# Real and imaginary parts on the same partitions, and a new passage between the two stages, in a two-block convolution kernel

## What is computed

```python
x = x + L0(_gn(x))    # per image: attention over 4 weight sets, 3x3 depthwise conv, 32x32 channel mix
x = x + L1(_gn(x))

# L1, with p = 8:
hidden = einsum('oc,bchw->bohw', w_hidden, x)            # 32 -> 192 channels
hidden = depthwise_conv_3x3(hidden, w_dw)
q, k, v = split(hidden, 3, axis=1)                       # 64 channels each
q_fft, k_fft = rfft2(8x8 patches of q), rfft2(8x8 patches of k)
out = irfft2(q_fft * k_fft)                              # circular convolution, patch by patch
out_norm = layernorm over the 64 channels of out, times norm_w plus norm_b
result = einsum('oc,bchw->bohw', w_out, v * out_norm)    # 64 -> 32 channels
```

## Time and profile before

| | us |
|---|---|
| median of 3 runs | 2588.41 (2576.62 to 2591.29) |
| the profiled execution: its own time | 2588.67 |
| its span in the profile | 2586.9 |
| PE busy | 2465.4 (95%) |
| DVE busy | 1638.6 (63%) |
| ACT busy | 1432.4 (55%) |
| mean granted share of PE's clock | 0.972 |

### The profile page before, as it was taken

One profiled execution on the slowest core, in us unless ns is written; L12 is line 12 of the kernel. 1 busy time (PEld: TensorE's weight loads), 2 busy tenths in 40 slices (PEclk: granted clock), 3 DMA queues, 4 the chain that ended last, 5 costly groups with the idle time before them and its releaser, 6 DMA issues.

```text
span 2586.9 us, 90657 instructions
## 1 busy us (share of the span) xinstructions
PE 2465.4 (95%) x40199; PEld 1644.8 (64%) x40199; DVE 1638.6 (63%) x4058; ACT 1432.4 (55%) x2381; POOL 476.5 (18%) x324
## 2 busy tenths in 40 slices
PE   6888988969999999999999999999999999999998
PEld 3333333357777777777777777777777777777775
DVE  3566766536666666666666666666666666666665
ACT  3455656555555555555555555555555555555552
POOL 1000000002222222222222222222222222222222
PEclk9888889879999999999999999999999999999999
DMA  7588898762222222222222222222222222233222
GB/s 139 147 210 214 219 237 215 195 155 69 68 69 69 69 69 68 69 69 69 69 68 69 69 69 69 68 69 69 69 69 68 69 69 68 71 74 74 72 52 50
DMA packets 60345, 248.30 MB, mean 96 GB/s; under 512 B 12393, under 2 KB 12658, under 8 KB 53714
## 3 DMA queue, kind: packets, MB, share of 16 engines
q1 hardware_dynamic: 59954, 242.50, 38.5%
HBM read 140.74 MB, written 101.72 MB: 94 GB/s over the span
## 4 chain that ended last, share of the span: by engine, by line
PE 76%; issue 1%; ACT 1%; DVE 0%; SPq 0%; DMA 0%; ACTq 0%
PE bank L575 21%; PE bank L652 18%; PE bank L668 10%; PE bank L558 9%; PE bank L635 8%; PE bank L588 6%; PE bank L597 4%; ACT arena L821 1%; SPq L318 0%; DMA xn_d<-arena 0%; DVE arena L1110 0%; DVE arena L961 0%; ACT arena L866 0%; DVE arena L1198 0%; DVE arena L1135 0%
## 5 line engine op out<-in xcount | busy, mean ns | idle before, releaser
L441 POOL TENSOR_TENSOR arena<-arena 128x8 f32<-128x8 f32 x256 | 452.2, 1766 | 1585.1 <-DVE arena L1116 1580.1
L575 PE MATMUL bank<-arena 128*64 128x512 f16 x4608 | 689.3, 393 | 0.0
L812 ACT ACTIVATE arena<-bank 100x512 f32<-100x512 f32 x1024 | 604.2, 628 | 95.8 <-PE bank L558 74.4
L1198 DVE TENSOR_TENSOR arena<-bank,arena 128x512 f32<-128x512 f32 x512 | 352.8, 691 | 432.3 <-PE bank L652 352.4
L652 PE MATMUL bank<-arena 100*64 100x128 f32 x8192 | 511.6, 274 | 13.7 <-issue 7.0
L652 PEld LDWEIGHTS bank<-arena 100*64 100x64 f32 x8192 | 455.9, 136 | 52.6 <-issue 45.6
L558 PEld LDWEIGHTS bank<-arena 128*36 128x36 f16 (+1 forms) x8192 | 327.8, 104 | 228.0 <-ACT arena L812 12.7
L512 PE MATMUL bank<-arena 32*32 32x508 f32 (+1 forms) x9216 | 391.7, 665 | 52.6 <-issue 37.7
L558 PE MATMUL bank<-arena 128*36 128x128 f16 (+1 forms) x8192 | 388.9, 220 | 11.0 <-DVE arena L1100 4.2
L858 ACT ACTIVATE arena<-bank 128x512 f32<-128x512 f32 x256 | 149.3, 598 | 343.8 <-PE bank L635 261.7
L821 ACT ACTIVATE arena<-bank,arena 128x256 f32<-128x256 f32 x512 | 261.0, 560 | 128.5 <-PE bank L588 127.9
(11 more groups left out here) (112 smaller groups left out, 1624.1 us busy)
## 6 DMA issues: line engine op xcount, KB each, us to landing
arena<-xn_d SPq DMA_DIRECT2D x128, 536.2 KB, 8.2
xn_d<-arena SPq DMA_DIRECT2D x130, 260.0 KB, 4.5
x_d<-arena SPq DMA_DIRECT2D x64, 512.0 KB, 8.3
arena<-x_d SPq DMA_DIRECT2D x128, 256.0 KB, 4.9
out<-arena SPq DMA_DIRECT2D x128, 256.0 KB, 5.4
arena<-x_in SPq DMA_DIRECT2D x32, 544.0 KB, 10.1
arena<-x_in SPq DMA_DIRECT2D x32, 528.0 KB, 10.0
arena<-spectra_in SPq DMA_DIRECT2D x1, 1152.0 KB
```

What stands on the lines that cost most here:

```text
L441: pool.tensor_tensor(tiny["rstd"][:, slot], tiny["var_eps"][:, slot], powers, ALU.pow).then_inc(s_root, 1)
L575: mm = pe.matmul(v_banks[chunk % 3][64 * s:64 * s + 64, :], v_w[:, 64 * tap:64 * tap + 64], at(xs[half], row * WP + 32 * k + dx, [32 * WP, ...
L812: act.activation(h_rows[0:WIN, :, first:first + 4], banks[g % ring][0:WIN, :].rearrange("p (i c) -> p c i", i=4), ACT.Copy).then_inc(s_h_r ...
L1198: dve.tensor_tensor(parts(prod[m % 3][:, 512 * second:512 * second + 512]), parts(k_banks[n % 3]), q_sb[m % 2][:, 256 * second:256 * secon ...
```

## The change

**Layout.** A real 8 x 8 patch has 64 independent real numbers as its spectrum. The new constants keep just these: row r of the first 32 and row r of the second 32 are the real and the imaginary part of one frequency (four rows hold purely real frequencies). So q and k both have 64 numbers a channel, in two parts of 32. In both octets a channel is two matmuls of 32 columns, and four channels stand beside each other on the four blocks of 32 partitions. Real and imaginary part of a channel stand on the same partitions, in different columns. DVE multiplies all four pairings (real by real, imaginary by real and so on) with instructions of the same size and number, 16 a unit. The inverse sums four matmuls of 32 rows instead of two of 64 rows, on four row tiles by two column tiles, for 16 channels at a time, into four banks. `G_k` and the table `spectra` are smaller, and `transform_step` makes 16 matmuls instead of 24.

**Order in the spectral part.** The k octet m now stands before q octet m+1. There is one q bank instead of two, and q octet m+1 waits until ACT has copied q octet m. There are two k banks of an octet each instead of three of a quad each. `project(tail, 3)` stands after q octet 2. `v_chunk(u, half, 0, 0, ...)` stands between the last k octet and the last inverse. ACT copies each inverse out in four pieces of 256 columns instead of two of 512, and does `turned_out(tail, 3, 1)` behind its first q copy instead of ahead of it. DVE does `gate(tail, 3, 1)` behind the first two products.

**Passage.** `high(14)` and `low(14)` stand ahead of unit 0's hidden work and of its first four windows. DVE's wait for the stores is gone, since the buffers of the spectral part no longer lie on the images' halves. The two `high(15)` are apart on ACT, and `load_xs(0, 1)` is issued earlier.

```diff
@@ PE, spectral part @@
-                    if positive(8 * u + m - 1):
-                        pe.wait_ge(s_q_copied, 8 * u + m - 1)
-                    for pair in range(4):
-                        for par in range(2):
-                            ch = 8 * m + 2 * pair + par
-                            mm = pe.matmul(banks[m % 2][64 * par:64 * par + 64, 128 * pair:128 * pair + 128],
-                                           G_q[0:WIN, 64 * ch:64 * ch + 64], hwin[0:WIN, 128 * ch:128 * ch + 128], start=True, stop=True)
+                    if positive(8 * u + m):
+                        pe.wait_ge(s_q_copied, 8 * u + m)
+                    for quad in range(2):
+                        for part in range(2):
+                            for c in range(4):
+                                ch, first = 8 * m + 4 * quad + c, 256 * quad + 128 * part
+                                mm = pe.matmul(q_bank[32 * c:32 * c + 32, first:first + 128],
+                                               G_q[0:WIN, 64 * ch + 32 * part:64 * ch + 32 * part + 32],
+                                               hwin[0:WIN, 128 * ch:128 * ch + 128], start=True, stop=True)
...
-                def inverse_octet(m):
-                    for part in range(2):
-                        for par in range(2):
+                def inverse(e):
+                    pe.wait_ge(s_prod_ready, 16 * u + 4 * e + 4)
+                    if positive(16 * u + 4 * e):
+                        pe.wait_ge(s_y_ready, 16 * u + 4 * e)
...
+                    for both in range(4):
+                        for c in range(4):
                             for lam in range(2):
-                                mm = pe.matmul(i_banks[par][64 * lam:64 * lam + 64, 256 * (m % 2):256 * (m % 2) + 256],
+                                mm = pe.matmul(i_banks[c][64 * lam:64 * lam + 64, 256 * (e % 2):256 * (e % 2) + 256],
...
@@ PE, hidden_group @@
-                if g < 2 and positive(8 * u):
-                    pe.wait_ge(s_q_copied, 8 * u)
+                if g == 0 and positive(16 * u):
+                    pe.wait_ge(s_prod_ready, 16 * u)
+                if g in (1, 2) and positive(16 * u):
+                    pe.wait_ge(s_y_ready, 16 * u - (3, 1)[g - 1])
@@ ACT, inverse_out @@
-                for par in range(2):
-                    act.activation(Y_out[:, 16 * e + par:16 * e + 16:2, :, :],
-                                   i_banks[par].rearrange("p (c s j) -> p c s j", s=2, j=32), ACT.Copy).then_inc(s_y_ready, 1)
+                if u == 0 and e == 0:
+                    act.wait_ge(s_xl_ready, 4 * NB)
...
+                for c in range(4):
+                    act.activation(Y_out[:, 16 * e + c:16 * e + 16:4, :, :],
+                                   i_banks[c][:, 256 * (e % 2):256 * (e % 2) + 256].rearrange("p (c s j) -> p c s j", s=2, j=32),
+                                   ACT.Copy).then_inc(s_y_ready, 1)
@@ DVE, before unit 0 @@
-            dve.wait_ge(s_xn_out, 128 * NB)
             spectral(0, None, (1, 1, 0))
```

More of the change, by code:

```diff
@@ L240, in build @@
         xq = [take(BAND * W) for _ in range(3)]
-        x2_1, x2_2, x2_0 = [take(QPIX) for _ in range(3)]
+        x2_1, x2_2 = [take(QPIX) for _ in range(2)]
+        conv_w = [take(9 * 32) for _ in range(2)]
+        first_image_free = top[0]
+        x2_0 = take(QPIX)
         x2 = [x2_0, x2_1, x2_2]
@@ L251, in build @@
         ones_row = take(128)
-        conv_w = [take(9 * 32) for _ in range(2)]
         st1, st2 = take(6 * NCH), take(6 * NCH)
@@ L352, in _ @@
                     load_x(later, (2, 3))
+                if b == NB + 1:
+                    load_xs(0, 1)
                 if older is not None:
@@ L557, in hidden_group @@
                     for low, high in ((0, 64), (64, WIN)):
-                        mm = pe.matmul(banks[g % ring][low:high, 128 * i:128 * i + 128], w[:, first + low:first + high], hidden_w,
+                        mm = pe.matmul(ring[g % len(ring)][low:high, 128 * i:128 * i + 128], w[:, first + low:first + high], hidden_w,
                                        start=True, stop=True)
@@ L637, in q_octet, with k_octet @@
                     mm.then_inc(s_q_mm, 1)
-                def k_quad(n, octet=None):
-                    if positive(16 * u + n - 2):
-                        pe.wait_ge(s_prod_ready, 16 * u + n - 2)
-                    if n == 1 and tail is not None:
+                def k_octet(m):
+                    if positive(16 * u + 2 * m - 2):
+                        pe.wait_ge(s_prod_ready, 16 * u + 2 * m - 2)
+                    if m == 0 and tail is not None:
                         pe.wait_ge(s_gated, 8 * u - 1)
-                    if n == 2 and tail is not None:
-                        pe.wait_ge(s_t_copied, 8 * u)
-                    for pair in range(2):
+                    for quad in range(2):
@@ L647, in k_quad @@
                         for part in range(2):
-                            if octet is not None and pair == 1 and part == 1:
-                                inverse_inputs(octet)
-                            for par in range(2):
-                                ch = 4 * n + 2 * pair + par
-                                mm = pe.matmul(k_banks[n % 3][64 * par:64 * par + 64, 256 * part + 128 * pair:256 * part + 128 * pair + 128],
-                                               G_k[0:WIN, 128 * ch + 64 * part:128 * ch + 64 * part + 64],
+                            for c in range(4):
+                                ch, first = 8 * m + 4 * quad + c, 256 * quad + 128 * part
+                                mm = pe.matmul(k_banks[m % 2][32 * c:32 * c + 32, first:first + 128],
+                                               G_k[0:WIN, 64 * ch + 32 * part:64 * ch + 32 * part + 32],
@@ L851, in spectral @@
             def spectral(u, tail):
-                if tail is not None:
-                    turned_out(tail, 3, 1)
                 for m in range(8):
@@ L857, in spectral @@
                         act.wait_ge(s_prod_ready, 16 * u + 2 * m - 2)
-                    act.activation(q_sb[m % 2], banks[m % 2], ACT.Copy).then_inc(s_q_copied, 1)
-                    if m % 2 == 1 and m >= 3:
+                    act.activation(q_sb[m % 2], q_bank, ACT.Copy).then_inc(s_q_copied, 1)
+                    if m == 0 and tail is not None:
+                        turned_out(tail, 3, 1)
+                    if m in (3, 5, 7):
                         inverse_out(u, m // 2 - 1)
@@ L1088, in _ @@
                 first_stats(later, range(3, NCH))
+            for i in range(4):
+                low(NB - 2, i)
             Y4 = Y.rearrange("p (s c j) -> p s c j", s=2, j=32)
```

179 lines of the change are left out of this document (86 added, 93 removed).

## The result

The changed kernel takes 2666.98 us (median of 4 runs, 2657.29 to 2687.61) against 2584.86 for the kernel before (4 runs): ratio 1.033, 95% interval 1.026 to 1.040. It is slower by 82 us at the medians. The profiled execution of the changed kernel is its longest run, 2687.61 us (span 2685.8), 99 us over the profiled one of before.

The account below looks back on a forecast made before the run. PE bounds the kernel, busy 95% of the span. Units at 59.2 + 7.4 us against 63.1 (+105), unit 31 -3.6, unit 0's turn +0.9, passage -11, start -9 gave +82 on 2588.7: 2670 us, range 2525 to 2765.

Parts of the forecast that it names:

- instructions come in time: Rival for stage 2: a late packet hides or the load lets packets in; 59.2 us a unit, 2449 us; chance 0.16.
- Octets and inverse: Spectral part: k octets 0.87 us instead of 1.75, 7.0 us a unit gained; q octets and inverse as before.
- The 36 ns of the earlier trace: Rival, spectral part: four column tiles at 36 ns a matmul, +6.4 us a unit of work, 2775 us; chance 0.05.
- the 62 ns: Sequencer cost per MATMUL by a skill rule: 47.6 us for the spectral part's 768 matmuls; given no chance.
- Spectral part without late packets: First q octet to last inverse: 31.3 - 7.0 + 2.2 + 0.4 = 26.9 us.
- Last inverse to turn: ACT's start on the last inverse to first turn: 6.8 us instead of 5.9, as ACT's copies take longer.
- Stand: Early in units 1 to 30: PE waits 4.8 us for a late instruction packet, from 7.2 to 12.0 us.
- Packets behind it: Instruction packets after the unit's late one stay tight: +0.5 us a unit, between 0 and 2.
- Clock: Half clock around each wait of PE loses 2.6 us a unit, between 0 and 5.1; rival, clock holds: 2593, chance 0.18.
- the waits swallowed: Spectral part: 0.5 us a unit of waits for ACT's copies, absorbed by PE's wait for the late packet.
- Start and passage: Start: fewer transforms and loads, -9 us (4 to 11). Passage: unit 0's spectral part ends 11 us earlier (5 to 16).
- Unit 31 and the end: The last unit, taken to have no load and so no late packets: -3.6 us.

Follow-up runs that it names:

- e4: Changed kernel without load_xs in units 1 to 30, which compute on the first two half images again; 2522.0 us, 0.976 of the kernel before.
- e7: Changed kernel with all transfers of a unit cut and spread, a second residual buffer and windows 0 to 3 later; 2420.9 us, 0.935 of the kernel before.
- e8: Kernel before, with PE waiting in each unit behind the first q octet for a chain of 13 small POOL memsets; 2799.6 us, ratio 1.082.
- e9: Changed kernel with only the residual's transfers moved (second residual buffer, store and load in pairs in the front); 2612.0 us, 1.009 of the kernel before.
- e1: Changed kernel with load_xs's 4 transfers cut into 16 pieces at the same place; 2575.2 us, 0.995 of the kernel before.
- e2: Changed kernel with load_xs in two parts, the second released after v's first chunk; 2544.8 us, 0.983 of the kernel before.
- e6: Kernel before, with two more transfers of 536 KB, which nobody reads, behind load_xs in each unit; 2589.6 us, ratio 1.000.
- e11: Kernel before, with two more transfers of 536 KB, which nobody reads, ahead of load_xs; 2588.7 us, ratio 1.001.

## Why the prediction was right

**Bound and mechanism.** Forecast 2670, measured 2667, by the mechanism named: packets late behind `load_xs`, the clock falling with the stand (e4, e7 and e8 show it). That the number is met within 3 us is partly luck: the terms below are read in the profiled execution, 2687.6 us, where +98.9 stands against the +82 forecast, and several terms missed in opposite directions. The rival "instructions come in time" (2449) is what e7 reaches by another edit.

**Octets and inverse.** Taken: 0.87 us an octet, 1.9 an inverse. Measured: 0.87 and 1.93 (899.59 to 901.52 in e7). The 36 ns of the earlier trace rows don't hold for four column tiles over 100 rows, so that rival falls. So do the 62 ns that the prediction takes from the Trainium skill for decoding in firmware: 32 recorded matmuls in 0.87 us are 27 ns each.

**Spectral part without late packets.** Sum 26.9 us, measured 26.9 in e7's unit 6.

**Last inverse to turn.** Taken 6.8, measured 5.8 (1641.80 to 1647.57): timeline of ACT in unit 16 of the changed kernel.

```profile
1641.80 1.21 ACT L870 ACTIVATE arena<-bank 128x256 f32<-128x256 f32 x4 [3.91 <-PE bank L679]
```

The step that failed is the price of a piece of 256 columns, taken as at most 0.51 us from `turned_out`: four together took 1.21 and not 2.04. DVE's statistics start at 1643.05, 1.25 us behind ACT's start and not 2.0, which is 0.75 of the 1.0; from there to the turn there are 4.5 us where 4.8 were taken, and why is open. Turn to q0: 25.5 as taken.

**Stand.** Taken: PE at the packet's end after 7.2 us, usable at 12.0, stand 4.8. In units 11 to 15 PE is there at 7.1 on average and goes on at 11.0: 3.9; over units 1 to 30 it is 7.5, 11.5 and 4.0. The mis-sized term is 12.0: in one unit of the five (11) PE could go on at 7.5 already. **Packets behind it**: taken 0.5, measured 1.3 (idle time of the changed kernel less that of e9); I had not counted the residual's transfers. **Clock**: taken 2.6, measured 3.3. Together with the waits swallowed 7.4 taken; 66.9 - 58.6 = 8.3 measured. And 59.2 without late packets was 58.6 in e7, mainly by the turn. The misses have opposite signs: 59.2 + 7.4 = 66.6 foreseen, 58.6 + 8.3 = 66.9 measured.

**Start and passage.** Timelines of the changed kernel: first convolution; DVE's first product of unit 0; a stand of PE in unit 0 and the inverse behind it; the hidden group behind the last inverse.

```profile
41.84 5.50 PE L522 MATMUL bank<-arena 32*32 32x512 f32 x160 [0.75 <-ACT arena L775]
```

```profile
544.34 1.28 DVE L1201 TENSOR_TENSOR arena<-bank,arena 128x512 f32<-128x512 f32 x2
```

```profile
563.76 1.08 PE L650 MATMUL bank<-arena 100*32 100x128 f32 x14 [2.63 <-issue]
564.77 3.72 PE L679 MATMUL bank<-arena 32*64 32x256 f32 x64
```

```profile
574.22 0.41 PE L570 MATMUL bank<-arena 128*64 128x128 f16 x8
```

Against the earlier trace rows: -9.8 for the start (9 taken), -19.7 at the first product, and -17.6 at the end of unit 0's spectral part, so -7.8 for the passage (11 taken, between 5 and 16). The first product came 9.9 us earlier by the passage, where I had taken 7; the step that failed is "unit 0 runs on warm". PE stood 2.63 us in it for nothing that the profile shows, and the inverse behind the stand took 3.72 us in place of 1.93. These sizes are those of one execution, though. Unit 1's first q octet comes at 605.7 here (623.4 before, -17.7), and at 592.5 to 601.7 in e1, e2, e4, e7 and e9, which have the same stage 1, passage and order: there start and passage together brought 22 to 31 us where 20 were taken.

**Unit 31 and the end.** Taken -3.6, measured +2.6. Timeline of PE in unit 31 (first q octet at 2612.59), in its third inverse and then behind the last one:

```profile
2634.98 3.24 PE L679 MATMUL bank<-arena 32*64 32x256 f32 x49 [1.91 <-issue]
```

```profile
2649.29 1.12 PE L602 MATMUL bank<-arena 128*128 128x128 f32 x4 [2.80 <-DVE arena L1137]
2650.34 4.05 PE L589 MATMUL bank<-arena 128*64 128x512 f16 x18
```

The last inverse ends 30.8 us after the first q octet and not 26.9: unit 31 has no `load_xs`, but it has the residual's transfers, and PE stands 1.91 us at 20.5 us and works slower behind it. In e9, with these transfers moved, there is no such stand and the inverse ends at 26.9. So the first turn comes 36.7 us after the first q octet, as before (36.9), and not 3.6 earlier. Then, with no hidden groups left and its first v chunk gone ahead, PE stands for 2.8 us, and the next chunk takes 4.05 us in place of 2.25; from the first turn to the end it takes 2.8 us more than before. I had taken unit 31 to be free of late packets, and carried the gain of k over without asking what PE has to do there.

**The sum** for the profiled execution: 30 x 3.8 = +113.9 (105), +2.6 (-3.6), -7.8 (-11), -9.8 (-9), unit 0's turn 0 (0.9): +98.9 against +82. The medians lie 82 apart.

## What to carry to other kernels

A kernel that splits matmuls pays in instructions: before you halve tiles, set the time in which PE uses up a packet (here 3.5 us in the spectral part) against the longest run of transfers that is queued at once. Long transfers are best cut and released one by one by the engines' progress, in the stretch where PE uses few instructions; that turned a loss of 3% into a gain of 6.5%. Stands of PE of 4 to 5 us cost half as much again in clock (2.5 on 4.7 in e8), or more (3.3 on 5.1 in the changed kernel). And a time that stays the same doesn't say that nothing moved: look in the trace for the event itself.

## What was not expected of the hardware

A packet of instructions is held up far less by more bytes in the queues than by longer transfer packets. 1.07 MB more, ahead of the load or behind it, changed no time and put the first packet of a unit 0.7 us later on average, 4.1 at the most (e6, e11), while the same bytes in packets of 4,420 in place of 17,160 bytes gave 92 us back (e1). And the clock: in each unit of e8, with its wait of 4.9 us, it stood at 0.50 for 6.8 us; in unit 8 PE worked in 4.25 of them, the rest was still the wait. The idle time of e7, 1.7 us a unit in shorter waits, left the clock at 1.00.
